# A state-space layer on one core: twelve of sixteen inflow steps by TensorE instead of ten, and the output projection moved into the next unit

## The reference

```python
u, z = jnp.split(x @ in_w.T, 2, axis=-1)
u = silu(sum(u_pad[:, k:k + L, :] * conv_w[:, k] for k in range(4)) + conv_b)
dbc = u @ xproj_w.T
dt = softplus(dbc[..., :dt_rank] @ dt_w.T + dt_b)
Bm, Cm = dbc[..., dt_rank:dt_rank + 16], dbc[..., dt_rank + 16:]
dA = exp(dt[..., None] * A)
dBu = (dt * u)[..., None] * Bm[:, :, None, :]      # the inflow of the change's name
# over tokens t:  h = dA_t * h + dBu_t ;  y_t = sum over the 16 states of h * C_t
return (y + u * D) * silu(z) @ out_w.T             # the output projection
```

## Time and profile before

| | us |
|---|---|
| median of 3 runs (lowest, highest) | 1371.97 (1368.11, 1373.04) |
| span of the profiled execution, its own time | 1397.4 |
| state-space part in it, about | 0 to 815 |
| TensorE, VectorE, GpSimd, ScalarE busy in it from 640 to 690 us | 48.78, 47.69, 48.87, 44.16 of 50 |

### The profile page before, as it was taken

One profiled execution on the slowest core, in us unless ns is written; L12 is line 12 of the kernel. 1 busy time (PEld: TensorE's weight loads), 2 busy tenths in 40 slices (PEclk: granted clock), 3 DMA queues, 4 the chain that ended last, 5 costly groups with the idle time before them and its releaser, 6 DMA issues.

```text
span 1397.4 us, 27753 instructions
## 1 busy us (share of the span) xinstructions
PE 1272.1 (91%) x9894; PEld 962.1 (69%) x9894; DVE 1097.7 (79%) x1829; ACT 947.2 (68%) x1630; POOL 1013.4 (73%) x620
## 2 busy tenths in 40 slices
PE   6799999999999999999998779999989999986695
PEld 2567767676777676766766646689966666656693
DVE  5799999999999999999999953333357888874475
ACT  5888988898889888988988842245545555532243
POOL 2789999999999999999999916223334665664442
PEclk9999999999999999999999999999999999998798
DMA  5545434543444454444444351312152000021223
GB/s 187 145 131 161 138 139 118 161 149 129 139 139 165 133 150 139 164 132 152 139 146 111 114 216 47 90 44 86 56 157 86 2 1 1 13 64 34 79 72 100
DMA packets 153014, 154.73 MB, mean 111 GB/s; under 512 B 96624, under 2 KB 121712, under 8 KB 143168
## 3 DMA queue, kind: packets, MB, share of 16 engines
q1 hardware_dynamic: 148112, 143.16, 32.8%
q0 software_dynamic: 4768, 9.81, 2.2%
HBM read 138.66 MB, written 20.20 MB: 114 GB/s over the span
## 4 chain that ended last, share of the span: by engine, by line
PE 49%; ACT 21%; DVE 16%; issue 8%; another core or an unknown queue 2%; DMA 2%; POOL 1%; SPq 1%; DVEq 1%; POOLq 0%; ACTq 0%
DVE hh L887 7%; PE pq L410 6%; ACT da L720 6%; PE pa L506 4%; PE py L525 3%; ACT pa L725 3%; PE bank L1562 3%; PE bank L1558 2%; PE pr L2016 2%; PE bank L1572 2%; PE pr L2219 2%; PE pr L2030 2%; PE bank L1478 2%; DVE hh L897 2%
## 5 line engine op out<-in xcount | busy, mean ns | idle before, releaser
L1042 POOL TENSOR_TENSOR hc<-hh,cs 128x1024 f32<-128x1024 f32 x256 | 596.9, 2369 | 24.6 <-DVE hh L887 21.7
L887 DVE TENSOR_TENSOR_SCAN hh<-da,st,pa 128x512 f32<-128x512 f32 x240 | 292.7, 1261 | 14.1 <-PE pa L506 12.6
L525 PE MATMUL py<-ident,hc 128*128 128x128 f32 x2048 | 268.4, 277 | 7.4 <-ACT yt L738 5.8
L525 PEld LDWEIGHTS py<-ident,hc 128*128 128x128 f32 x2048 | 229.1, 141 | 54.4 <-issue 29.1
L506 PEld LDWEIGHTS pa<-dg,dtut 64*128 64x128 f32 x2560 | 160.9, 189 | 107.0 <-issue 103.2
L506 PE MATMUL pa<-dg,dtut 64*128 64x128 f32 x2560 | 189.8, 285 | 29.6 <-DVE hh L887 20.6
L720 ACT ACTIVATE da<-dt,w 128x512 f32<-128x512 f32 x320 | 209.7, 711 | 0.2
L897 DVE TENSOR_TENSOR_SCAN hh<-pa,st,hh 128x512 f32<-128x512 f32 x144 | 175.2, 1265 | 6.1 <-POOL hh L1032 3.7
L725 ACT ACTIVATE pa<-dt,w 128x512 f32<-128x512 f32 x192 | 124.5, 680 | 35.2 <-DVE hh L887 20.8
L410 PE MATMUL pq<-xn,w 128*128 128x512 f32 x248 | 124.6, 627 | 3.6 <-ACT xn L755 3.6
L1032 POOL TENSOR_TENSOR hh<-dtu,bs 128x1024 f32<-128x1024 f32 x48 | 112.8, 2365 | 3.1 <-issue 1.9
(11 more groups left out here) (341 smaller groups left out, 2643.8 us busy)
## 6 DMA issues: line engine op xcount, KB each, us to landing
cs<-bcrows SPq DMA_DIRECT2D x64, 1024.0 KB, 4.9
dg<-blocks SPq DMA_DIRECT2D x80, 256.0 KB, 5.0
bs<-bcrows SPq DMA_DIRECT2D x48, 256.0 KB, 3.7
blocks<-bcrows SPq DMA_DIRECT2D x320, 1.0 KB, 3.2
xsorted<-in_pads SPq DMA_DIRECT2D x13, 387.0 KB, 5.7
rot<-in_rot SPq DMA_DIRECT2D x4, 1024.0 KB, 4.9
wx<-in_l_w SPq DMA_DIRECT2D x4, 1024.0 KB, 10.0
ysort<-ytoken SPq DMA_DIRECT2D x14, 256.0 KB
```

The lines of the kernel that those rows point to most:

```text
L525: i = pe.matmul(py[:, h * CH + kt * P:h * CH + (kt + 1) * P], hc[s % HCS][:, h, t], ident[:, :], is_transpose=True, start=n == 0 and kt == ...
L887: v.tensor_tensor_scan(hh[(NS * m + nj) % HHS][:, h, :], da[q % DAS][:, :], inflows, 0.0 if first else st[:, m % 2, nj, h:h + 1], ALU.mult ...
L1042: g.tensor_tensor(hc[s % HCS][:, :, :], hh[s % HHS][:, :, :], cs[j % 2][:, s % CG, :].unsqueeze(1).broadcast_to([P, HF, CH]), ALU.mult).th ...
```

## The change

- BY_G goes from (0, 1, 7) to (0, 1), BY_V from (4, 10, 13) to (4, 13). BY_P has 12 steps: pairs (2,3), (5,6), (7,8), (9,10), (11,12), (14,15).
- B's rows for VectorE's steps are no longer spread by TensorE. A DMA puts the row on all partitions of a new tile `brow` (`b_row_in`), and ScalarE copies it into `pb` (`spread_b`, L737 there), in steps 0 and 8.
- Six block pairs instead of five, with 24 small scattering DMAs a unit instead of 20; the ring `da` of decays has 6 tiles instead of 4.
- `out_project` of unit m - 2 runs in steps 1 and 2 of unit m (before: of unit m - 1 in steps 8 and 9), and `add_out` follows scan 2. It holds for units up to 12 (`late_out`); 13 and 14 keep the old place. The statistics of a finished chunk follow in steps 7 and 8 instead of 13 and 14.

```diff
-BY_G = (0, 1, 7)
-BY_V = (4, 10, 13)
+BY_G = (0, 1)
+BY_V = (4, 13)
+SPREAD_AT = (0, 8)
-SLOTS, DAS, BG = 4, 4, 2
+SLOTS, DAS, BG, BVS = 4, 6, 2, 2
...
                     def x_project(m):
                         pe.wait_ge(s_uz, first_count(m))
+                        if m >= 3:
+                            pe.wait_ge(s_om, m - 2)
...
+                        if m >= 3 and late_out(m - 3) and n in (1, 2):
+                            out_project(m - 3, ((0, 1), (2, 3))[n - 1])
-                        if m >= 2 and m - 2 < UNITS - 1 and n in (8, 9):
+                        if m >= 2 and m - 2 < UNITS - 1 and not late_out(m - 2) and n in (8, 9):
                             out_project(m - 2, ((0, 1), (2, 3))[n - 8])
...
-                        if s + 2 < STEPS and by_vector(s + 2):
-                            spread_b(s + 2)
...
+                    def spread_b(s):
+                        m = s // NS
+                        k = made(BY_V, s) - 1
+                        act.wait_ge(s_brow[k % BVS], 16 * (k // BVS + 1))
+                        if k >= 1:
+                            act.wait_ge(s_db, k)
+                        act.wait_ge(s_turnk, turned_count(m, HF - 1))
+                        act.activation(pb[:, :], brow[k % BVS][:, :], ACT.Identity).then_inc(s_b, 1)
...
+                        if s % NS in SPREAD_AT:
+                            spread_b(s // NS * NS + BY_V[SPREAD_AT.index(s % NS)])
...
+                        if n == 2 and m >= 2 and late_out(m - 2):
+                            add_out(m - 2)
+                        if n == 7 and m >= 2 and late_out(m - 2):
+                            chunk_stats(m - 2)
...
-                        if n == 9 and m >= 1:
+                        if n == 9 and m >= 1 and not late_out(m - 1):
                             add_out(m - 1)
...
+                    def b_row_in(k):
+
+                        m = k // len(BY_V)
+                        sy.wait_ge(s_cout, 16 * (m + 1))
+                        if k >= BVS:
+                            sy.wait_ge(s_b, k - BVS + 1)
+                        sy.dma_start(brow[k % BVS][:, :], bcrows[m][BY_V[k % len(BY_V)], :].partition_broadcast(P)).then_inc(s_brow[k % BVS], 16)
...
                     load_block(0)
+                    for i in range(len(BY_V)):
+                        b_row_in(i)
```

More of the change, by code:

```diff
@@ L103, in build @@
         s_phase = sem("phase_done")
+        s_back = [sem(f"b_row_in_then_back_in{i}") for i in range(4)]
+        back0 = [16 * (UNITS * len(BY_V) // BVS) if i < BVS else 0 for i in range(4)]
         phases = [0]
@@ L232, in layer0_mamba @@
                 keep = sb(k, "keep", [P, NCH + len(SQUARES) + 1])
-                sel = sb(k, "sel", [P, NS])
+                brow = [sb(k, f"brow{i}", [P, CH]) for i in range(BVS)]
                 pre = sb(k, "pre", [P, 4, CH])
@@ L247, in layer0_mamba @@
                 cs = [sb(k, f"cs{i}", [P, CG, CH]) for i in range(2)]
-                bs = [sb(k, f"bs{i}", [P, BG, CH]) for i in range(2)]
+                bs = [sb(k, f"bs{i}", [P, BG, CH]) for i in range(-(-len(BY_G) // BG))]
                 da = [sb(k, f"da{i}", [P, CH]) for i in range(DAS)]
@@ L348, in kept_states, with late_out @@
                     return NS * sum(followed(m) for m in range(s // NS)) + (s % NS + 1 if followed(s // NS) else 0)
+                def late_out(m):
+                    return m < UNITS - 3
                 def made(by, s):
@@ L475, in prep @@
                             z_half(m, n - 14)
[L477 to L482, removed]
                     def turn_dtu(m, h):
@@ L918, in chunk_stats, with chunk_moments @@
                             vector_stats(range(t.start, t.stop))
+                    def chunk_moments(m):
+                        if is_second(m):
+                            t = tiles_of_chunk(m)
+                            vector_moments(range(t.start, t.stop))
                     def start_stats(part, tiles):
@@ L996, in mamba_vector @@
                             negated(1)
-                        if n == 9 and m >= 1:
+                        if n == 2 and m >= 2 and late_out(m - 2):
+                            add_out(m - 2)
+                        if n == 7 and m >= 2 and late_out(m - 2):
+                            chunk_stats(m - 2)
+                        if n == 8 and m >= 2 and late_out(m - 2):
+                            chunk_moments(m - 2)
+                        if n == 9 and m >= 1 and not late_out(m - 1):
                             add_out(m - 1)
-                        if n == 13 and m >= 1:
+                        if n == 13 and m >= 1 and not late_out(m - 1):
                             chunk_stats(m - 1)
-                        if n == 14 and m >= 1 and is_second(m - 1):
-                            t = tiles_of_chunk(m - 1)
-                            vector_moments(range(t.start, t.stop))
+                        if n == 14 and m >= 1 and not late_out(m - 1):
+                            chunk_moments(m - 1)
                         if n == LAG + 1 and m >= 1:
@@ L1154, in mamba_sync @@
                                 diagonals_out(i)
-                        if len(BY_G) > BG:
-                            b_in(m, 1)
                         if m == 0:
[L1158 to L1161, removed]
+                            diagonals_in(1)
+                        diagonals_in(m * len(PAIRS) + 2)
+                        diagonals_in(m * len(PAIRS) + 3)
                         c_in(4 * m + 2)
@@ L1164, in mamba_sync @@
                             rows_out(m + 1)
-                        if m >= 1:
-                            for i in range(DGS, len(PAIRS)):
-                                diagonals_in(m * len(PAIRS) + i)
+                        diagonals_in(m * len(PAIRS) + 4)
                         if m + 1 < UNITS:
                             b_in(m + 1, 0)
+                            b_row_in((m + 1) * len(BY_V))
                             for i in range(2):
@@ L1190, in build @@
         s_xsort, s_scat, s_ret = sem("sorted_in"), sem("scattered"), sem("returned")
-        s_back = [sem(f"back_in{i}") for i in range(4)]
         s_back0 = sem("first_back_in")
@@ L2821, in constants @@
     k["centre"] = np.eye(D, dtype=np.float32) - np.float32(1.0 / D)
-    k["sel"] = (np.arange(P)[:, None] == np.arange(NS)).astype(np.float32)
     k["before"] = np.triu(np.ones((P, P), np.float32), 1).astype(mybir.dt.np(BF16))
```

27 lines of the change are left out of this document (14 added, 13 removed).

## The result

The changed kernel takes 1424.53 us, median of 4 runs (1421.74 to 1426.33); the kernel before, run beside it, 1370.04 (1364.98 to 1373.04). The ratio is 1.0405, 95% interval 1.0377 to 1.0434: slower, near the 1420 predicted and inside the range.

What follows compares the result with a forecast made beforehand. The prediction took a loop through three engines, period 47.69 us, to bound the kernel. Steady units 43.6, units 0 and 1 1.9, unit 15 -1.1 and start 3.6 sum to 48.0; from 1371.97 that gives 1420 us, range 1390 to 1434.

Steps and rivals of the forecast that it cites:

- The bound: A loop through three engines, not the nearly full engines themselves, sets the unit's period of 47.69 us.
- I12 to I2: From TensorE's inflow of step 12 to the next unit's inflow of step 2: no instruction added or removed, 17.11 us stay.
- I2 to I6: TensorE's inflow of step 2 to that of step 6: VectorE waits 2.05 us at `add_out`; 15.07 us, 2.41 more.
- I6 to I12: TensorE's inflow of step 6 to that of step 12: later second dt projection delays ScalarE's decays; 18.86 us, 0.94 more.
- The copy in step 0: ScalarE's new copy in step 0: hidden by the wait at `add_out`; without it, step 4's decays come 0.50 us later.
- The period: One steady unit, the loop's three stretches summed: 51.04 us against 47.69, 3.35 more, in units 2 to 14.
- Unit 0: Start: added scattering DMAs and rows of B before a block load cost 3.6 us; later dt projection costs 0.94.
- Unit 1: Has no late output projection, so only the 0.94 us of the stretch from step 6 to step 12.
- Unit 15: Last unit, prepares nothing and is led by VectorE: loses the inflow of step 10, a gain of 1.1 us.
- counts decide: Rival: TensorE's and GpSimd's occupancy sets the period, so the unit falls 1.1 us to 46.6; 1356 us, chance 0.09.
- About no change: Rival: ScalarE is not narrow between inflows 6 and 12, so VectorE wins 1.68 us there; 1384 or 1374 us, chance 0.09.
- Late blocks: Rival: block loads wait for all 24 scattering DMAs, 2 us more in each of 13 units; 1446 us, chance 0.05.

Runs made afterwards that it cites:

- both orders mended: The changed kernel with both output projection halves in step 1 and the second dt projection ahead of step 7's inflow: 1373.79 us, ratio 1.0028.
- the first kernel: The changed kernel with the late output projection off, so the projection and `add_out` return to steps 8 and 9: 1403.13 us, ratio 1.0258.

## Why the prediction was right, by its steps

- **The bound.** Right. Three engines busy 95 to 98% were not the limit: they fell to 86 to 90% and the kernel slowed by 4%. With both orders mended GpSimd is busy 222.53 us of the 240 from 500 us, where before it was 234.76, and the period is 47.45 instead of 47.69: 0.24 us a unit is all that the change buys then.
- **I12 to I2**, 17.11: measured 17.11.
- **I2 to I6**, 15.07: measured 15.15. The wait at `add_out` was given as 2.05 and is 2.01. With both halves in step 1 it is gone, and I2 to I6 falls to 13.42.
- **I6 to I12**, 18.86: measured 19.04. The scans of step 9 start 11.29 us after I6 instead of 11.12. Of that, 0.14 is that the two A between I6 and the dt projection take 1.02 to 1.03 each from start to start, not 0.955. The extra wait of step 10, 0.43, is 0.30.
- **The copy in step 0** was said to be hidden by `add_out`, and to cost 0.50 without it. Right that it is hidden: doubled under cover it left the period at 51.30. Uncovered (the first kernel) it cost 0.75 a unit, half as much again as said: it starts 0.72 us after the copy of `dtut`, not 0.50.
- **The period**, 51.04: measured 51.30. Over units 2 to 14 that is 47.1 us (GpSimd's step 11 goes from 5.37 us late in unit 1 to 52.51 in unit 14), against 43.6 predicted.
- **Unit 0**: 3.18 us, against 3.6 + 0.94 = 4.54. The number is low only because the first scan starts 1.85 us earlier in this profile, which the prediction had at nothing and the runs don't tie to the change. VectorE's first scans, before and then after:

```profile
42.00 4.65 DVE L897 TENSOR_TENSOR_SCAN hh<-pa,hh 128x512 f32<-128x512 f32 x4 [2.54 <-POOL hh L1032]
```

```profile
40.15 4.64 DVE L910 TENSOR_TENSOR_SCAN hh<-pa,hh 128x512 f32<-128x512 f32 x4 [2.54 <-POOL hh L1055]
```

From there to step 11 unit 0 grew by 5.03: 0.7 ahead of step 4, 2.85 for the late block (3.6 said), and 1.5 after it (0.94 said).
- **Unit 1**: 2.19 us against 0.94. It has no late output projection, so nothing covers the copy in step 0. The prediction had a price for that and didn't apply it here; the first kernel's units, built alike, grew by 2.01.
- **Unit 15**: 2.15 us, where a gain of 1.1 stood. This is the one term with the wrong sign. Its `add_out` is in the old place, after scan 9. Rows of VectorE in unit 15, before and then after:

```profile
769.76 2.46 DVE L897 TENSOR_TENSOR_SCAN hh<-pa,st,hh 128x512 f32<-128x512 f32 x2 [0.96 <-ACT pa L725]
...
776.62 2.45 DVE L887 TENSOR_TENSOR_SCAN hh<-da,st,pa 128x512 f32<-128x512 f32 x2 [0.17 <-PE pa L506]
...
787.16 0.66 DVE L912 SCALAR_TENSOR_TENSOR residual<-residual,pq 128x512 f32<-128x512 f32 x1
```

```profile
823.10 2.46 DVE L910 TENSOR_TENSOR_SCAN hh<-pa,st,hh 128x512 f32<-128x512 f32 x2 [1.70 <-ACT pa L727]
...
830.52 9.48 DVE L900 TENSOR_TENSOR_SCAN hh<-da,st,pa 128x512 f32<-128x512 f32 x8 [0.73 <-PE pa L511]
...
841.79 0.69 DVE L925 SCALAR_TENSOR_TENSOR residual<-residual,pq 128x512 f32<-128x512 f32 x1 [1.79 <-PE pq L465]
```

`add_out` waits 1.79 us for O halves that now stand behind more inflows, step 4 waits 0.74 more, and step 6 waits 0.56 more for its inflow: TensorE's granted clock is 0.50 (1.2 GHz) from 824 to 828 us, after it had waited 1.89 us, and 1.00 in the four us before step 6 in the other profile. Less the 1.1 for the inflow of step 10 these make 2.0 of the 2.15. VectorE leads this unit, so nothing covers them. The wait at `add_out` is also what broke the expectation of the dt projection first without the late output projection.

The sum: 3.18 + 2.19 + 47.14 + 2.15 - 0.20 (behind the last step 11) = 54.46, against 48.0. The mechanism was right at each place of the loop; the 6.5 us that were short are 3.5 in the steady units, 3.25 in unit 15 and 1.25 in unit 1, less 1.36 at the start and 0.2 at the end. Counted from the first scan it is 56.3, and 8.3 short: the early first scan made the forecast look better than its terms were.

**The rivals.** That counts decide fell with the first reading: GpSimd's busy time fell from 48.87 to 43.06 of 50, and the unit grew. About no change needed ScalarE not to be the narrow place of I6 to I12: VectorE did lose `add_out` and an inflow there, and waited 2.86 us for decays instead. Only with the dt projection ahead did that stretch fall, to 16.92, one us under the 17.92 of before. Late blocks showed in unit 0 alone, although the 30 us of slack that the prediction set against them stand in none of its rows: SP's 243.0 us of waiting in 550 are some 21 us a unit. ScalarE's rows after give the table loads again: from 681.85 to 685.61, two loads and the sigmoid between them, 3.76 us, with 1.29 and 1.30 from the start of a load to the next instruction. The Trainium skill (ScalarE: Activation LUTs, "What ACT_TABLE_LOAD costs") has 2.66 us for each switch, 5.3 for two. The trace does not agree.

## What to carry to other kernels

When several in-order engines are nearly full, cut the period at one recurring instruction and sum the legs: a moved step costs what it delays at the one consumer that comes to it too early, not its own length. After any change of order look at every consumer of that kind, in the first, second and last unit too, where a cover is missing. Gains of two edits add up only where neither wait was the other's cover.

## What was not expected of the hardware

TensorE's granted clock fell after short waits in some units and not in others, with the same instructions and the same wait. With the late output projection alone TensorE waited 1.75 to 2.24 us at one inflow in each of the units 2 to 13, and the clock fell in four of the twelve, after 1.86 to 1.87 us, at 1.64 us each; after the two longest waits of these, 2.23 and 2.24 us (at 424 and 373 us), it stayed at 1.00. With the copy in step 8 doubled it waited 1.67 to 1.72 us in units 1 to 13, and the clock fell in four of these thirteen, at 1.5 each. In the changed kernel, whose waits from 200 to 750 us are 1.54 us at most, it did in none of them. In each of the eight `pq<-xn,w`, 1.98 us at 2.4 GHz, took 3.05 to 3.47. Late in unit 14 TensorE waits 3.53 us in both kernels, and the inflow behind it takes 2.08 us instead of 1.16. So a wait on TensorE can cost more than itself, and the length of the wait alone does not decide it. What decides in which units the clock falls, these runs don't show.
